# Joining and scaling the attention context ahead of the output product, in a four-layer transformer kernel

## The reference, cut to what matters

```python
q = (x @ q_proj_w.T).reshape(b, s, 16, 192)            # 128 nope + 64 rope
compressed = x @ kv_a_proj_w.T                         # 64 latent + 64 rope
kv = rmsnorm(compressed[..., :64], kv_a_ln_w) @ kv_b_proj_w.T
k = concat(kv[..., :128] per head, k_rope); v = kv[..., 128:] per head
probs = softmax(where(causal, q @ k.T * 192**-0.5, -1e9))
out = concat_heads(probs @ v) @ o_proj_w.T
x = layernorm(x + out)
```

## Time and profile before

| | us |
|---|---|
| runs | 817.57, 813.15, 811.64; median 813.15 |
| the profiled execution | 812.66, span 810.9 |
| PE busy | 768.1 (95%) |
| DVE busy | 555.0 (68%) |
| ACT busy | 397.7 (49%) |
| POOL busy | 309.7 (38%) |
| attention loop in the trace | about 78 to 408 of the span |
| granted TensorE clock, mean | 0.995 |

### The profile page before, as it was taken

How to read it: one execution, slowest core, us unless ns; L and a number is a source line. 1 busy time by engine, 2 the same in 40 slices (tenths; PEclk the granted TensorE clock), 3 DMA queues, 4 the chain that set the end, 5 groups by cost and what they waited for, 6 DMA issues and landing times.

```text
span 810.9 us, 16066 instructions
## 1 busy us (share of the span) xinstructions
PE 768.1 (95%) x4619; PEld 652.6 (80%) x4619; DVE 555.0 (68%) x1401; ACT 397.7 (49%) x899; POOL 309.7 (38%) x408
## 2 busy tenths in 40 slices
PE   8999989999999999999989999889999999999997
PEld 7887867777778788777778999788887888888885
DVE  5323778787868778777746666468858388888546
ACT  1234656656656566566514444313343266666431
POOL 2004446443433333322345665625444233333341
PEclk9999999999999999999999999999999999999999
DMA  7349971000000000009238899777651234555331
GB/s 215 100 112 340 404 296 46 29 29 28 24 26 23 21 22 22 21 15 327 87 104 296 282 363 362 267 267 278 242 184 72 72 94 153 152 152 155 111 111 52
DMA packets 61282, 120.75 MB, mean 149 GB/s; under 512 B 18016, under 2 KB 30816, under 8 KB 61088
## 3 DMA queue, kind: packets, MB, share of 16 engines
q1 hardware_dynamic: 52864, 96.59, 35.9%
q0 software_dynamic: 8352, 23.34, 8.0%
HBM read 76.13 MB, written 43.78 MB: 148 GB/s over the span
## 4 chain that ended last, share of the span: by engine, by line
PE 71%; DVE 10%; issue 8%; DMA 4%; POOL 3%; ACT 3%; SPq 1%; DVEq 0%; ACTq 0%; POOLq 0%
PE scores L1673 9%; PE scores L1675 9%; PE scores L1674 9%; PE scores L1897 6%; PE acc_ps L2093 5%; PE misc_ps L1803 4%; PE misc_ps L1801 4%; PE probsT_ps L1788 3%; PE probsT_ps L1810 3%; PE scores L1907 3%; PE probsT_ps L2027 3%; PE acc_ps L1788 3%; DVE xT_lo L1139 2%; DVE neg_max L1133 2%; PE probsT_ps L1886 1%
## 5 line engine op out<-in xcount | busy, mean ns | idle before, releaser
L868 ACT ACTIVATE area<-scores,neg_max 128x128 f32<-128x128 f32 (+7 forms) x128 | 94.9, 742 | 86.3 <-DVE neg_max L1133 85.9
L1133 DVE TENSOR_REDUCE neg_max<-scores 128x1 f32<-128x128 f32 (+7 forms) x128 | 95.8, 749 | 21.8 <-PE scores L1760 21.7
L711 POOL DMA_INDIRECT xe_d<-x_rows,send_i x64 | 64.0, 1001 | 55.3 <-ACT x_rows L892 38.5
L751 POOL DMA_INDIRECT ye_d<-area,home_i x64 | 61.4, 959 | 39.1 <-DVE home_i L1340 18.4
L699 POOL CAST weff_hi<-area 128x256 fp32r<-128x256 f32 x42 | 16.6, 395 | 135.1 <-PE scores L1760 87.5
L1673 PE MATMUL scores<-kT_hi,weff_hi 128*128 128x512 f32 (+3 forms) x172 | 66.6, 387 | 0.9 <-ACT area L845 0.4
L1897 PE MATMUL scores<-area 128*96 128x128 f32 x512 | 66.4, 273 | 0.4 <-issue 0.4
L1675 PE MATMUL scores<-kT_hi,weff_lo 128*128 128x512 f32 (+3 forms) x172 | 61.5, 358 | 0.0
L1674 PE MATMUL scores<-kT_lo,weff_hi 128*128 128x512 f32 (+3 forms) x172 | 61.4, 357 | 0.0
L1803 PE MATMUL misc_ps<-xT_lo,xT_hi 128*128 128x512 f32 x144 | 58.3, 405 | 1.9 <-DVE xT_lo L1139 1.8
L1897 PEld LDWEIGHTS scores<-area 128*96 128x96 f32 x512 | 59.2, 163 | 0.7 <-issue 0.6
(11 more groups left out here) (308 smaller groups left out, 2069.8 us busy)
## 6 DMA issues: line engine op xcount, KB each, us to landing
area<-w SPq DMA_DIRECT2D x23, 512.0 KB, 4.2
area<-gate_up SPq DMA_DIRECT2D x24, 384.0 KB, 5.1
xe_d<-area SPq DMA_DIRECT2D x8, 1088.0 KB, 11.4
ye_d<-area SPq DMA_DIRECT2D x8, 1024.0 KB, 16.9
area<-w SPq DMA_DIRECT2D x8, 1024.0 KB, 7.6
area<-ye_d SPq DMA_DIRECT2D x15, 512.0 KB, 5.0
area<-xe_d SPq DMA_DIRECT2D x28, 272.0 KB, 6.1
area<-down SPq DMA_DIRECT2D x24, 192.0 KB, 6.6
```

The source lines that it names most:

```text
L711: pool.indirect_dma_start(xe_d, bass.IndirectOffsetOnAxis(send_i[:, t, k:k + 1], 0), x1_rows[:, t, :], None).then_inc(sent[k % 2] if t < T ...
L868: act.activation(row_of(n)[:, 0:L], score_bank(n)[:, 0:L], ACT.Exp, bias=neg_max[:, n % 4:n % 4 + 1], accum_out=rsum[:, s, k:k + 1]).then_ ...
L1133: dve.tensor_reduce(neg_max[:, n % 4:n % 4 + 1], score_bank(n)[:, 0:(n // HEADS + 1) * P], AX.X, ALU.max, negate=True).then_inc(max_ready, 1)
```

## The change

The context's two halves are joined before the output product, so that a head needs 64 partitions and two heads fit in one contraction. ACT no longer copies the context as it is: `cross_ctx` copies partitions 64 to 127 of the first two heads to partitions 0 to 63, and partitions 0 to 63 of the last two heads to 64 to 127. DVE adds the other half (`join_ctx`). `wvo` has heads 0 and 1 of a group on the lower half and heads 2 and 3 on the upper one. The product contracts head j with head j + 2, and the two products of a group add up in PSUM, so the softmax scaling can't be applied afterwards: DVE writes each reciprocal 64 times (`invert`, now 256 elements per partition), PE transposes that (`spread_scales`), and DVE multiplies the joined context by it (`scale_ctx`). One addition per group is left (`add_out`). A semaphore counts join, join, scale and addition of a group (`joined_at(G)` = 4G + 2, `scaled_at(G)` = 4G + 3, `added_at(G)` = 4G + 4), another scales and output (2G + 1, 2G + 2). The transposed input comes in two halves, the second by ACT's queue, as do the norm's weights; DVE splits it in four instructions.

```diff
--- before.py
+++ after.py
...
@@ -94,7 +93,7 @@
         weff = cutA3(2, HC, P)
         weff_hi = sb("weff_hi", [P, 2, HC, P], f32r)
         weff_lo = sb("weff_lo", [P, 2, HC, P], f32r)
-        wvo = cutA3(HEADS * HID)
+        wvo = cutA3(PAIRS * HID)
         qT = area1
         q_hi = sb("q_hi", [P, 2, P], f32r)
         q_lo = sb("q_lo", [P, 2, P], f32r)
@@ -109,10 +108,11 @@
         pT_hi = [xT_hi[:, 0, 0:BANK], xT_hi[:, 0, BANK:], xT_lo[:, 1, 0:BANK]]
         pT_lo = [xT_lo[:, 0, 0:BANK], xT_lo[:, 0, BANK:], xT_lo[:, 1, BANK:]]
         rsum = sb("rsum", [P, 3, QUAD])
-        rinv = sb("rinv", [P, 3, QUAD])
+        rinv = cutA3(3, 2, P)
         y = sb("y", [P, HID])
         sgd = sb("sgd", [P, 2, BANK])
-        ctxT = sgd
+        ctx_joined, ctxT = (sgd[:, :, part * HID:(part + 1) * HID] for part in range(2))
+        LOW, HIGH = slice(0, RANK), slice(RANK, P)
         stats = sb("stats", [P, 6])
         mv = sb("mv", [P, TILES, 2])
         rstd = sb("rstd", [P, TILES])
...
@@ -418,14 +415,15 @@
             return route_places.get((G % SETS, place)) if SETS + 2 <= G < GROUPS else None
         tenants = []
-        for G in range(GROUPS + 1):
+        for G in range(GROUPS + 2):
             for spot in range(8):
                 if route_at(G, spot):
                     tenants.append((route_at(G, spot), tile_of(G) - 1))
                 tenants += [("block", b) for b in blocks_at(G - 1, spot)]
-                if spot % 2 and 0 <= G - 2:
-                    tenants.append(("out", QUAD * (G - 2) + spot // 2))
-        tenants += [("out", QUAD * (GROUPS - 1) + i) for i in range(QUAD)]
+                if spot == 5 and 0 <= G - 2:
+                    tenants.append(("out", G - 2))
+                if spot == 7 and 0 <= G - 1 < GROUPS:
+                    tenants.append(("scales", G - 1))
         tenants += [(what, TILES - 1) for what in route_places.values()]
         def seat(what, n):
@@ -433,7 +431,7 @@
             return tenants.index((what, n))
         LENT = pT + [acc, half[3]] + half[0:3]
-        long_rows = seat("out", TWO_OUTS)
+        long_rows = seat("scales", SHORT // QUAD - 3) + 1
         tail = seat("block", blocks_to(GROUPS - 1))
         def seats_in_turn():
...
@@ -494,12 +507,13 @@
                     body(G, i, QUAD * G + i)
+        xT_v = xT.rearrange("(c p) t -> p c t", p=P)
+
         @block.sync
         def _(sp):
-            sp.dma_start(xT_in[:], xT.rearrange("(c p) t -> p c t", p=P)).then_inc(ld_xT, 16)
+            sp.dma_start(xT_in[:, :, 0:BANK], xT_v[:, :, 0:BANK]).then_inc(ld_xT[0], 16)
             sp.dma_start(wkv_a[:], wkv_aT.rearrange("(c p) n -> p c n", p=P)).then_inc(ld_kv, 16)
             sp.dma_start(wkb[:], wkv_b.rearrange("(h a p) r -> a p h r", a=2, p=P)[0]).then_inc(ld_head[0], 16)
-            sp.dma_start(lnw[:], bass.AP(kv_ln.tensor, 0, [[0, P], [1, RANK]])).then_inc(ld_head[1], 16)
             wq_v = wq.rearrange("(h d) n -> d h n", d=QDIM)
             wr_v = wq_ropeT.rearrange("(c p) (h r) -> p c h r", p=P, h=HEADS)
             wv_v = wkv_b.rearrange("(h a p) r -> a p h r", a=2, p=P)[1]
@@ -830,6 +844,8 @@
         @block.scalar
         def _(act):
+            act.dma_start(xT_in[:, :, BANK:], xT_v[:, :, BANK:]).then_inc(ld_xT[1], 16)
+            act.dma_start(lnw[:], bass.AP(kv_ln.tensor, 0, [[0, P], [1, RANK]])).then_inc(ld_head[1], 16)
             act.wait_ge(kv_ready, 1)
             act.activation(sq[:], banks[1][:].rearrange("p (t n) -> p t n", t=TILES)[:, :, 0:RANK],
                            ACT.Square).then_inc(sq_done, 1)
@@ -874,11 +890,12 @@
                     act.wait_ge(ctx_step, b - 2)
                 act.activation(pT_hi[b % 3], seat_of("block", b)[:], ACT.Copy).then_inc(hi_done, 1)
-            def copy_ctx(G):
+            def cross_ctx(G):
                 act.wait_ge(ctx_step, blocks_to(G + 1))
                 if G >= 2:
-                    act.wait_ge(out_ready, QUAD * (G - 1))
-                act.copy(ctxT[:, G % 2, :], ctx_ps[:]).then_inc(ctx_copied, 1)
+                    act.wait_ge(ctx_used, scaled_at(G - 2))
+                act.copy(ctx_joined[LOW, G % 2, :], ctx_ps[HIGH, 0:HID]).then_inc(ctx_crossed, 1)
+                act.copy(ctx_joined[HIGH, G % 2, :], ctx_ps[LOW, HID:]).then_inc(ctx_crossed, 1)
             def copy_x1T(t):
                 act.wait_ge(x1T_psd, t + 1)
...
@@ -1076,10 +1093,15 @@
         @block.vector
         def _(dve):
-            dve.wait_ge(ld_xT, 16)
-            dve.tensor_copy(xT_hi[:], xT_in[:]).then_inc(x_split, 1)
-            dve.wait_ge(x_split, 1)
-            dve.tensor_tensor(xT_lo[:], xT_in[:], xT_hi[:].bitcast(f32), ALU.subtract).then_inc(x_split, 1)
+            x_halves = [slice(0, BANK), slice(BANK, T)]
+            for b, part in enumerate(x_halves):
+                dve.wait_ge(ld_xT[b], 16)
+                dve.tensor_copy(xT_hi[:, :, part], xT_in[:, :, part]).then_inc(x_split, 1)
+            for b, part in enumerate(x_halves):
+                dve.wait_ge(x_split, b + 1)
+                dve.tensor_tensor(xT_lo[:, :, part], xT_in[:, :, part], xT_hi[:, :, part].bitcast(f32),
+                                  ALU.subtract).then_inc(x_split, 1)
+
             def split_weff(h, u, i):
                 dve.wait_ge(weff_f32, h + 1)
...
@@ -1117,16 +1139,17 @@
                 dve.wait_ge(k_split, 2 * b + 1)
                 dve.tensor_tensor(kT_lo[:, part], acc[:], kT_hi[:, part].bitcast(f32), ALU.subtract).then_inc(k_split, 1)
-            wvo_copy(0)
+            wvo_copy(0, 0, LOW)
             split_keys(0)
             split_weff(2, 0, 1)
             split_weff(3, 1, 1)
             split_keys(1)
-            wvo_copy(1)
-            with dve.Fori(2, PAIRS) as j:
-                split_weff(2 * j, 0, j)
-                split_weff(2 * j + 1, 1, j)
-                wvo_copy(j)
+            wvo_copy(1, 0, HIGH)
+            with dve.Fori(1, SETS) as s:
+                for b, rows in enumerate((LOW, HIGH)):
+                    split_weff(4 * s + 2 * b, 0, 2 * s + b)
+                    split_weff(4 * s + 2 * b + 1, 1, 2 * s + b)
+                    wvo_copy(2 * s + b, s, rows)
             def row_max(n):
                 dve.wait_ge(scores_ready, n + 1)
@@ -1141,20 +1164,35 @@
             def invert(G):
                 dve.wait_ge(probs_ready, QUAD * (G + 1))
-                dve.reciprocal(rinv[:, G % 3, :], rsum[:, G % 3, :]).then_inc(rinv_done, 1)
-
-            def add_head(n):
-
-                t, h = divmod(n, HEADS)
-                s, k = stat_of(n)
-                dve.wait_ge(out_ready, n + 1)
-                if h == 0:
+                wide = [P, 2, 2, RANK]
+                dve.reciprocal(rinv[:, G % 3].rearrange("p j (b r) -> p j b r", b=2),
+                               rsum[:, G % 3, :].rearrange("p (b j) -> p j b", b=2).unsqueeze(3).broadcast_to(wide)
+                               ).then_inc(rinv_done, 1)
+
+            def join_ctx(G):
+
+                dve.wait_ge(ctx_crossed, 2 * G + 2)
+                for rows, part in ((LOW, slice(0, HID)), (HIGH, slice(HID, 2 * HID))):
+                    dve.tensor_tensor(ctx_joined[rows, G % 2, :], ctx_ps[rows, part], ctx_joined[rows, G % 2, :],
+                                      ALU.add).then_inc(ctx_used, 1)
+
+            def scale_ctx(G):
+
+                dve.wait_ge(scales_and_out, scales_at(G))
+                dve.wait_ge(ctx_used, joined_at(G))
+                dve.tensor_tensor(ctxT[:, G % 2, :], seat_of("scales", G)[:, 0:HID], ctx_joined[:, G % 2, :],
+                                  ALU.mult).then_inc(ctx_used, 1)
+
+            def add_out(G):
+
+                t = tile_of(G)
+                dve.wait_ge(scales_and_out, out_at(G))
+                if G % SETS == 0:
                     dve.wait_ge(ld_x, 32)
-                    dve.wait_ge(rinv_done, n // QUAD + 1)
                 else:
-                    dve.wait_ge(out_read, n)
-                dve.scalar_tensor_tensor(x1[:, t, :], out_of(n), rinv[:, s, k:k + 1], x1[:, t, :] if h else x_in[:, t, :],
-                                         ALU.mult, ALU.add).then_inc(out_read, 1)
+                    dve.wait_ge(ctx_used, added_at(G - 1))
+                dve.tensor_tensor(x1[:, t, :], seat_of("out", G)[:, 0:HID], x1[:, t, :] if G % SETS else x_in[:, t, :],
+                                  ALU.add).then_inc(ctx_used, 1)
             def variance(k, src, eps, s=0):
@@ -1174,7 +1212,7 @@
                 return normalise(k, src, dst)
             def attention_variance(t):
-                dve.wait_ge(out_read, (t + 1) * HEADS)
+                dve.wait_ge(ctx_used, added_at(SETS * t + SETS - 1))
                 variance(t, x1[:, t, :], LN_EPS)
             def finish_tile(t):
@@ -1255,9 +1293,11 @@
                     if routed and at in ((3, 2), (3, 3)):
                         next(places[t], None)
-                behind = n - 1 - 2 * QUAD
-                if 0 <= behind < TILES * HEADS:
```

(52 more changed lines are left out.)

31 lines of the change are left out of this document (19 added, 12 removed).

## The result

The changed kernel took 853.95 us (median of 4 runs, 849.06 to 856.72) beside 813.28 us for the kernel before on the same chip: ratio 1.0493 [1.0433, 1.0553]. The forecast was no change, 813.5 us; the time lies above the range, 22 us over its upper end. Slower had 0.31 of the chances, of which the third rival (830 us) held most.

The account below looks back on a forecast made before the run. The prediction read PE, 95% busy, as what bounds the kernel, with DVE limiting small tiles; its terms, -3.7 + 9.0 + 1.0 - 5.1 - 0.4 = +0.8 on 812.66, gave 813.5 us, range 798 to 832.

Parts of the forecast that it names:

- the third rival: Attention stage: the reciprocal's block on DVE stalls PE once per group at the first context product; 830 us, chance 0.27.
- PE, 0.64 us less per group: Output products: two fewer, two transposes more per group; 20.5 us in 32 groups if PE were the only limit.
- The fourth rival: Whole change: the PE work isn't worth its time and nothing else is either; 812 us, inside the forecast, no separate chance.
- DVE, the reciprocal: DVE, per group: the reciprocal of 256 elements takes 2.3 us where 4 elements took 0.167.
- The first rival: DVE: the large reciprocal costs like any operation, 0.43 us; 791 us, chance 0.13.
- Floor per tile: Attention tiles: none shorter than its DVE work or than now minus 2.56; +8.4 and -12.1, sum -3.7 us.
- Delay behind the reciprocal: Tiles 3 to 7: PE waits for the remainder copy queued behind it, 0.45 us in each of 20 groups; +9.0 us.
- Context's way: Context to output: ACT's two copies, then DVE's joins, delay PE and make DVE wait; +1.0 us, bounds 0 and 19.
- Fewer tenants: PSUM banks: two tenants per group instead of four halve PE's waits at block transposes; -5.1 us, bounds 0 and -10.2.
- Prologue: Start: two loads leave SP's queue for ACT's, so head weights may come sooner; -0.4 us, bounds +0.5 and -1.1.
- Tail: After the last context copy: 3.8 us where there were 3.6, counted as nothing.

Follow-up runs that it names:

- e9: The kernel before, with half the columns left out of three of four heads' output products (less PE work); 809.37 us, ratio 0.9943.
- e10: The kernel before, with the reciprocal written 64 times per head but cut into four pieces, one at the end of each of four head slots; 822.7 us.
- e5: The kernel before, with only the reciprocal written 64 times per head in one block, as in the changed kernel; 842.89 us, ratio 1.0357.
- e1: The changed kernel, with a short reciprocal of 4 elements and then a DVE copy repeating it 64 times; 835.01 us, ratio 1.0274.
- e8: The e3 kernel without DVE's joins, the context's remainder half left out of the output; 810.11 us, ratio 0.9962.
- e2: The changed kernel, long reciprocal kept, with PE's spreading of the scales and DVE's scaling moved a slot later, next to each other; 832.93 us, ratio 1.026.
- e4: The kernel before, with only the loads changed: input in halves, two loads by ACT's queue, DVE's split in four instructions; 811.32 us, ratio 0.9985.
- e3: The changed kernel with both edits: short reciprocal plus 64-fold DVE copy, and the later spreading and scaling; 815.68 us, ratio 1.0012.
- e7: The e3 kernel, with the 64-fold copy of the reciprocals made by POOL instead of DVE; 809.62 us, ratio 0.9952.
- e12: The kernel before, with half the columns left out of three of four heads' output products and scaled additions (PE and DVE); 807.01 us, ratio 0.9906.
- e11: The kernel before, with half the columns left out of three of four heads' scaled additions (less DVE work only); 810.33 us, ratio 0.9959.

## Why the prediction was wrong, by its own steps

**PE, 0.64 us less per group.** The passes went as counted (128 of the output and 64 transposes for 256), but "if PE were the only limit" was then carried into the floor as "now minus 2.56" for tiles 4 to 7 and -1.9 for tile 3, -12.1 in all, from PE's share of 95%. e9 gives 5.3 for that cut in these tiles. A step that failed: busy time had been taken for the bound. The fourth rival had this right.

**DVE, the reciprocal.** The mechanism was right and the size 0.6 us too large: 1.742 for 2.3. The first rival (0.43) is out, and with it the view that a large one runs like any operation.

**Floor per tile.** This step failed most. It put +8.4 on tiles 0 to 2; measured +22.0. DVE's work came out below the forecast (17.88 us for 19.8 in tile 0, 27.51 for 29.7 in tile 1), and the tiles still ended 3 to 7 us above their floors. A floor assumes that DVE's idle time can be used up first. It can when the work comes in small pieces (e10: 16.77 of 18.9, 31.05 of 33.3, close to full), not when it is one block ahead of a row maximum (e5). The stretches of lower clock are part of it as well, up to 8.5 us in these three tiles by their mean clocks.

**Delay behind the reciprocal, +9.0** in tiles 3 to 7: e5 measured +8.9 there, and e1 took 6.5 away. The size agrees, by luck. The step had PE wait at the context product for the remainder copy; in e5 that wait grew from 0.9 to 2.7 us. And by its own reading a reciprocal of 1.742 us starts the copy at 314.49 only 0.53 us later, inside tile 6's 0.90 us of room. What grew by 8.5 us is ACT's wait for the row maximum, which the step names in passing ("and then the row maximum, for which ACT's exponential waits") and puts no price on. No such reading was made for the small tiles; the working says "where DVE's load isn't already counted". There it was needed most.

**Context's way, +1.0.** e8 puts the joins at 4 us, inside the bounds of 0 and 19 and above the value taken. "The scaling needs PE's transposed reciprocals, issued a slot earlier: nothing" is the sentence in which the large miss sits. Issued earlier was taken as harmless for who reads; it was not asked what the result occupies until it is read.

**Fewer tenants, -5.1.** The sign was wrong, and its bounds of 0 and -10.2 left out a loss. Two tenants are fewer than four, but one of them now stays for 3.9 us. PE's waits at the block transposes went from 10.2 us to 30.1; undoing that is worth 21 us (e2), 14.2 of it in tiles 3 to 7. With -5.1 expected, this one step accounts for most of what tiles 3 to 7 cost against the forecast.

**Prologue, -0.4:** +0.4 in the profile, and e4 shows no effect. Both readings of SP's hold had been given; it moved. **Tail, nothing:** what follows the attention stage is 2.2 us shorter, which no experiment explains; the same stretch varies from 403.9 to 408.5 us among the kernels.

**The rivals.** The third named a real loss, a DVE block in front of what PE needs, but in tiles 3 to 7 at the first context product. It is the small tiles that pay most, by way of the row maximum and ACT, and the second half of the loss belongs to no rival.

The parts, against the kernel before: block reciprocal in place of the short one and its copy together with the held bank +38 (e3 against the changed kernel; 17 to 19 and 19 to 21 of it), joins +4, the copy on DVE +5 (e3 against e7, by the ratios), PE's work -4.6, loads -1. They make +41 or so for a measured 40.7. The joins, the copy and the loads are each uncertain by 2 to 3 us, and no run isolates the scaling and the one addition that stand for four scaled additions (1.06 us of DVE's work less per group) or ACT's second copy, which the sum leaves out. So the closeness is partly luck.

## What to carry to other kernels

An engine's busy share prices nothing by itself. Before costing an added instruction, follow what stands behind it in its queue and on to the next engines until the path comes back; if it does, the block is paid nearly whole, and it can be cut into pieces, which gave back 21 of 29 us here with no work less, or given to an idle engine (5 us for the copy). For every buffer that a change fills earlier, ask when its reader gets to it and who needs the place meanwhile. PE's work in such a loop is worth a fraction of its time (here a fifth to two fifths), and that can be measured beforehand by leaving some out.

## What the runs showed of the hardware

**The reciprocal on DVE** costs 167 ns for 4 elements a partition, 543 for 64 and 1742 for 256: 6.3 ns an element over both steps, where a copy of 256 takes 294 ns in all. The small sizes on which I had leaned grow by 8.3 to 9 ns an element, which made my value too large. The Trainium skill, "VectorE: DVE Perf Modes", section "First, the fixed hardware budget", has a repeat of 8, an estimated 8.3 ns an element at the page's 0.96 GHz; the measured slope is six such cycles. That the operation repeats, and doesn't stream, the runs bear out; the count they don't.

**PE's clock** was at 1.00 in the attention stage's windows before. In the changed kernel it fell in tile 0 (windows; PEclk is the third number from the end):

```profile
78.00:81.00 3.00, 2.17 (x14) 1.44 (x13) 2.42 (x4) 1.29 (x5) 2.76 (x5) 1.00 1.03 397
81.00:84.00 3.00, 2.62 (x15) 2.62 (x15) 1.69 (x6) 2.13 (x7) 0.41 (x2) 0.60 1.04 394
84.00:87.00 3.00, 3.00 (x11) 2.56 (x11) 3.00 (x6) 0.81 (x4) 1.84 (x3) 0.50 1.05 401
87.00:90.00 3.00, 3.00 (x22) 2.85 (x21) 1.69 (x6) 2.23 (x7) 0.41 (x2) 0.76 1.05 414
```

PE was idle for 0.8 of the first 3 us, then ran at the lower level of 1.2 GHz, 0.50, for nearly 7 us by these windows' means. At that level the four output passes at 85.75 took 1.91 us, and those at 112.39 2.02; all the others take 1.02 to 1.13. From the mean clocks of the eight windows PE spent some 24 us at the lower level (window length x (1 - PEclk) x 2), so up to 12 us of the 38.6 by which these windows grew may be this, if none of it fell into waits.

In the profiled executions it fell in tile 0 or 1 also in e1, e2, e3, e5, e9 and e12, but not in e4, e7, e8, e10 or e11. In tile 0 this need not be the edit's doing. A window of e5 (its first long reciprocal starts at 79.97), and a window and the first lighter output product of e9:

```profile
77.00:78.00 1.00, 1.00 (x8) 1.00 (x6) 0.29 (x1) 0.58 (x3) 0.92 (x3) 0.51 1.04 407
...
78.00:80.00 2.00, 2.00 (x13) 2.00 (x11) 0.39 (x2) 1.06 (x3) 1.84 (x5) 0.50 1.04 400
...
83.82 0.74 PE L1811 MATMUL acc_ps<-area,sgd 128*128 128x128 f32 x2
```

In both PE was at the lower level before the edited instructions began. The clock also differs between executions of one kernel, and the time with it: among the runs of the kernel before beside these experiments, seven at a mean clock of 0.989 took 815.7 us on average and six at 0.997 took 811.4. The changed kernel's four were at 0.976 to 0.981, e5's at 0.983 to 0.987, e10's at 0.991 to 0.995. What decides when it falls stays open.
